# Attention on one Trainium2 core: three key banks, one bank for values and sums, and row maxima carried by two DMAs through DRAM

## The reference

```python
q = (layernorm(x) @ Wq + bq)          # heads of 32, scaled by 32 ** -0.5
k = (ctx @ Wk + bk);  v = (ctx @ Wv + bv)
attn = softmax(clip(q @ k.T, -1e4, 1e4))
x = x + tanh(g_xattn) * ((attn @ v) @ Wo + bo)
x = x + tanh(g_ffn) * (h + 0.5 * (silu(norm(h) @ w1 + b1) @ w2 + b2))   # h = layernorm(x); w1, w2 dequantised
```

## Time and profile before

| | us |
|---|---|
| Median of 3 runs | 3423.44 (3421.34 to 3423.89) |
| The profiled execution, its own time | 3422.4 |
| Its span in the profile | 3420.6 |
| First and last turn of row maxima (L708) | 491.0 and 2439.3 |
| PE busy over the span | 3212.1 (94%) |
| DVE / ACT / POOL busy over the span | 2032.0 / 1603.2 / 1909.7 |

### The profile page before, as it was taken

How to read it: one execution, slowest core, us unless ns; L and a number is a source line. 1 busy time by engine, 2 the same in 40 slices (tenths; PEclk the granted TensorE clock), 3 DMA queues, 4 the chain that set the end, 5 groups by cost and what they waited for, 6 DMA issues and landing times. The chain is left out here.

```text
span 3420.6 us, 51826 instructions
## 1 busy us (share of the span) xinstructions
PE 3212.1 (94%) x15941; PEld 1871.3 (55%) x15941; DVE 2032.0 (59%) x2788; ACT 1603.2 (47%) x2847; POOL 1909.7 (56%) x897
## 2 busy tenths in 40 slices
PE   6799979999999999999999999999656699999999
PEld 5688844444444444444444444444244588888887
DVE  8766656666666666666666666666469433333332
ACT  2222226666666666666666666666522111111111
POOL 4666537777777777777777777777554000000000
PEclk9899979999999999999999999999978899999999
DMA  5566672212222122212222122221195100000000
GB/s 170 187 209 213 213 223 57 56 39 54 56 56 51 42 56 56 55 46 47 56 56 55 41 53 56 56 51 43 57 279 176 40 25 25 25 25 25 15 14 22
DMA packets 142086, 263.11 MB, mean 77 GB/s; under 512 B 16961, under 2 KB 57921, under 8 KB 134721
## 3 DMA queue, kind: packets, MB, share of 16 engines
q1 hardware_dynamic: 141344, 253.82, 26.1%
q10 hardware_dynamic: 672, 8.39, 0.8%
HBM read 168.84 MB, written 93.32 MB: 77 GB/s over the span
## 5 line engine op out<-in xcount | busy, mean ns | idle before, releaser
L852 DVE TENSOR_REDUCE at_half_max<-ps 128x1 f32<-128x1024 f32 x1024 | 1245.0, 1225 | 635.0 <-PE ps L671 623.3
L790 ACT ACTIVATE at_probT<-ps 128x512 f32<-128x512 f32 x2048 | 1113.2, 595 | 418.6 <-PE ps L688 364.4
L620 POOL TENSOR_TENSOR at_gp_sum<-at_gp_sum,at_probT 128x1024 f32<-128x1024 f32 x512 | 1218.3, 2380 | 42.4
L671 PE MATMUL ps<-at_k_stack,at_q_stack 96*128 96x512 f32 x2048 | 868.2, 425 | 19.8 <-DMA at_k_stack<-kT_hi 18.2
L688 PE MATMUL ps<-at_q_stack,at_k_stack 98*128 98x512 f32 x2048 | 876.8, 429 | 9.3 <-ACT at_probT L790 3.4
L671 PEld LDWEIGHTS ps<-at_k_stack,at_q_stack 96*128 96x128 f32 x2048 | 390.1, 191 | 392.9 <-DVE at_half_max L852 202.0
L688 PEld LDWEIGHTS ps<-at_q_stack,at_k_stack 98*128 98x128 f32 x2048 | 385.8, 189 | 351.2 <-ACT at_probT L790 319.1
L615 POOL TENSOR_TENSOR at_gp_sum<-at_probT 128x1024 f32<-128x1024 f32 x128 | 304.9, 2382 | 431.9 <-ACT at_probT L790 431.9
L725 PE MATMUL ps<-at_probT,at_v_head 128*32 128x512 f32 x4096 | 542.4, 601 | 0.9 <-ACT at_probT L790 0.9
L1361 ACT ACTIVATE ff_y<-ps,ff_b_t 128x512 f32<-128x512 f32 x128 | 88.2, 689 | 612.8 <-PE ps L1324 612.8
L1376 POOL TENSOR_TENSOR ff_x_in<-ff_x_in,ff_b_half 128x2048 f32<-128x2048 f32 x8 | 36.8, 4602 | 601.6 <-DVE ff_x_in L1398 601.6
(11 more groups left out here) (154 smaller groups left out, 3890.2 us busy)
## 6 DMA issues: line engine op xcount, KB each, us to landing
at_k_stack<-kT_hi SPq DMA_DIRECT2D x128, 256.0 KB, 4.9
kT_hi<-kv_k_hi SPq DMA_DIRECT2D x16, 1024.0 KB, 4.2
kT_lo<-kv_k_lo SPq DMA_DIRECT2D x16, 1024.0 KB, 6.5
v_heads<-kv_v_out SPq DMA_DIRECT2D x16, 1024.0 KB, 5.7
at_q_stack<-qT_hi SPq DMA_DIRECT2D x128, 128.0 KB, 3.3
at_k_stack<-kT_lo SPq DMA_DIRECT2D x64, 256.0 KB, 4.3
at_v_head<-v_heads SPq DMA_DIRECT2D x64, 256.0 KB, 5.0
kv_c_in<-in_ctx_dram SPq DMA_DIRECT2D x16, 768.0 KB, 7.1
```

Of the source, the lines that this page charges most:

```text
L620: pool.tensor_tensor(gp_sum[lane % 2][:, :, :], gp_sum[lane % 2][:, :, :], pairs[:, 2 * i + 2:2 * i + 4, :], ALU.add).then_inc(gp_added, 1)
L671: mm = pe.matmul(ps[:, n, :], q_stack[buf][0:PARTS, rows], k_stack[buf][0:PARTS, BANK * n:BANK * (n + 1)], start=True, stop=True)
L790: act.activation(probT[lane % 2][:, kv, :], src, ACT.Exp).then_inc(exp_done, 1)
L852: dve.tensor_reduce(dst, src, AX_X, ALU.max).then_inc(max_done, 1)
```

## The change

Four things change in `attend`, on the path without clipping:

1. Key products take turns on three banks, 4, 5 and 6, in place of two. Each waits for the exponential of the key product three before it.
2. Values and sums share bank 7. Two rounds of `values` stand in one slot (C) and two in the next (D). `fold` and three of the sums (`fold_values`) stand in the next slot A, and the last three sums in the slot B after it. There are as many of these products as before.
3. The turn of the row maxima on TensorE and the copy on ScalarE are gone. SP writes `neg_hi` to a DRAM tensor, element by element (128 partitions x 8 elements of 4 bytes), waits until that has landed, and issues a second DMA that reads it back as 2 rows of 512 elements into `q_stack`. The first key product of the unit waits for that DMA (`row_loaded`).
4. The key products of a unit begin one slot later than before (`KEYS` 7 in place of 6). `attend` runs one slot more at its end.

```diff
-    TURN, KEYS, PV, FOLD = 5, 6, 7, 12
+    TURN, KEYS, PV, SUMS, FOLD = 6, 7, (10, 11), 12, 13
+    RING = 3
+    def key_bank(lane, kv):
+        return 4 + (KVT * lane + kv) % RING
...
+            def turn_maxima(head, slot, half):            # on SP
+                unit = HALVES * head + half
+                sp.wait_ge(split_done, 5 * (unit + 1))
+                sp.dma_start(neg_d[bass.ds(unit, 1)].rearrange("u t b p -> p (u t b)"),
+                             neg_hi[:, :, :].bitcast(F32).rearrange("p t b -> p (t b)"), allow_slow_non_contiguous=True).then_inc(neg_moved, 16)
+                sp.wait_ge(neg_moved, 16 * (unit + 1))
+                rows = q_stack[slot][PARTS:PARTS + 2, BANK * half:BANK * (half + 1)]
+                sp.dma_start(rows.bitcast(F32).rearrange("b (t p) -> b t p", p=P),
+                             neg_d[bass.ds(unit, 1)].rearrange("u t b p -> b (u t) p")) \
+                    .then_inc(row_loaded, 16)
...
+                if (n := at(base, slot, 2, BUFS, N_HEADS)) is not None:
+                    turn_maxima(n, (slot - 2) % BUFS, 1)   # after the loads of a head
...
+                if (n := at(base, slot, 1, BUFS, N_HEADS)) is not None:
+                    turn_maxima(n, (slot - 1) % BUFS, 0)   # after the stores of a head
...
-                    pe.wait_ge(row_copied, unit + 1)
-                need(pe, exp_done, KVT * unit + kv - 1)
+                    if clipping:
+                        pe.wait_ge(row_copied, unit + 1)
+                    else:
+                        pe.wait_ge(row_loaded, 16 * (unit + 1))
+                need(pe, exp_done, KVT * unit + kv - RING + 1)
...
-                need(act, fold_done, unit)
-                act.copy(partial[:, :], ps[:, 6, :]).then_inc(partial_done, 1)
+                need(act, partial_read, unit)
+                act.copy(partial[:, :], ps[:, 7, :]).then_inc(partial_done, 1)
...
             def step(base, slot):                          # TensorE
                 scores(base, slot, 0)
                 keys(base, slot, 0)
                 scores(base, slot, 1)
                 keys(base, slot, 1)
-                fold(base, slot)
-                for r in range(QT):
-                    values(base, slot, PV + r, (r,))
+                spread_maxima(base, slot)                  # with clipping alone
+                values(base, slot, PV[0], (0, 1))
+                values(base, slot, PV[1], (2, 3))
+                fold_values(base, slot)
                 last_sums(base, slot)
-                turn_maxima(base, slot)
                 scores(base, slot, 2)
                 keys(base, slot, 2)
                 scores(base, slot, 3)
                 keys(base, slot, 3)
```

More of the change, by code:

```diff
@@ L582, in attend @@
         split_done = sem("split_done")
+        neg_moved = sem("neg_moved")
+        row_loaded = sem("row_loaded")
         row_turned = sem("row_turned")
@@ L683, in keys, with spread_maxima @@
                 if kv == 0:
-                    pe.wait_ge(row_copied, unit + 1)
-                need(pe, exp_done, KVT * unit + kv - 1)
+                    if clipping:
[3 more added lines that the diff above has]
+                need(pe, exp_done, KVT * unit + kv - RING + 1)
                 q = BANK * (lane % HALVES)
-                pe.matmul(ps[:, 4 + kv % 2, :],
+                pe.matmul(ps[:, key_bank(lane, kv), :],
                           k_stack[buf][0:rows, P * kv:P * (kv + 1)], q_stack[buf][0:rows, q:q + BANK],
                           start=True, stop=True).then_inc(tile_done, 1)
-            def turn_maxima(base, slot):
+            def spread_maxima(base, slot):
                 unit, lane, r = unit_at(base, slot, TURN)
-                if unit is None or r:
+                if unit is None or r or not clipping:
                     return
@@ L701, in turn_maxima @@
                     cols = slice(P * t, P * (t + 1))
[L702 to L709, removed]
+                    for part in range(2):
+                        mm = pe.matmul(ps[:, 7, cols], wide[:, part, t, :], ident_r[:, :],
+                                       start=(part == 0), stop=(part == 1))
                 mm.then_inc(row_turned, 1)
@@ L721, in values @@
                     pe.wait_ge(v_loaded[buf], 16 * n_loads + 16)
-                    need(pe, partial_done, unit)
+                    need(pe, gather_done, unit)
+                    if clipping and not (isinstance(unit, int) and unit + 1 >= UNITS):
+                        pe.wait_ge(row_copied, unit + 2)
                 for r in rounds:
                     for g in range(4):
-                        mm = pe.matmul(ps[D * g:D * (g + 1), 6, :], v_head[buf][:, 4 * r + g, :],
+                        mm = pe.matmul(ps[D * g:D * (g + 1), 7, :], v_head[buf][:, 4 * r + g, :],
                                        probT[lane % 2][:, 4 * r + g, :], start=(r == 0), stop=(r == QT - 1))
@@ L728, in values, with fold_values, last_sums @@
                     mm.then_inc(pv_done, 1)
-            def last_sums(base, slot):
-                unit, lane, r = unit_at(base, slot, PV + QT - 1)
+            def fold_values(base, slot):
+                unit, lane, r = unit_at(base, slot, SUMS)
                 if unit is None or r:
                     return
-                need(pe, gather_done, unit)
+                pe.wait_ge(partial_done, unit + 1)
+                pe.matmul(ps[0:D, 7, :], A["fold"][:, :], partial[:, :], start=True, stop=True)
                 for g in range(1, 4):
-                    pe.matmul(ps[D * g:D * (g + 1), 7, :], ones[:, :], probT[lane % 2][:, KVT - 5 + g, :],
-                              start=True, stop=False)
-            def fold(base, slot):
+                    mm = pe.matmul(ps[D * g:D * (g + 1), 7, :], ones[:, :], probT[lane % 2][:, KVT - 5 + g, :],
+                                   start=True, stop=False)
+                mm.then_inc(partial_read, 1)
+            def last_sums(base, slot):
                 unit, lane, r = unit_at(base, slot, FOLD)
@@ L793, in copy_maxima @@
                 unit, lane, r = unit_at(base, slot, TURN)
-                if unit is None or r:
+                if unit is None or r or not clipping:
                     return
                 act.wait_ge(row_turned, unit + 1)
[L797 to L803, removed]
+                need(act, shift_done, KVT * (unit - 1))
+                act.copy(neg_rows[lane % 2][:, :], ps[:, 7, :]).then_inc(row_copied, 1)
             def copy_partial(base, slot):
-                unit, lane, r = unit_at(base, slot, PV + QT - 1)
+                unit, lane, r = unit_at(base, slot, PV[1])
                 if unit is None or r:
@@ L867, in split_maxima @@
                     need(dve, row_turned, unit)
+                    need(dve, neg_moved, 16 * unit)
                     dve.tensor_scalar(neg_hi[:, :, 0], row_max[:, :], -1.0, None, ALU.mult).then_inc(split_done, 1)
@@ L878, in split_maxima @@
                     dve.tensor_reduce(neg_pair[:, :, 1].bitcast(F32R), pair, AX_X, ALU.max).then_inc(split_done, 1)
-                    need(dve, row_turned, unit)
+                    need(dve, neg_moved, 16 * unit)
                     dve.tensor_reduce(neg_hi[:, :, 0], pair, AX_X, ALU.max, negate=True).then_inc(split_done, 1)
```

14 lines of the change are left out of this document (8 added, 6 removed).

## The result

The changed kernel takes 4149.68 us (median of 4 runs, 4143.28 to 4158.2) against 3423.66 of the kernel before: 1.2124 times the time, 95% interval 1.2099 to 1.2148. I had forecast 3289, faster, with a range of 3264 to 3352. It is slower by 726 us, beyond even the 3690 of the rival that I had put on that side.

A forecast was written before the change was run, and what follows sets the result against it. PE was taken as the bound, losing time to two key banks. -1.0 (ring), -0.24 (turn) and +0.16 (VectorE) a unit, times 128, plus 4 us for start and end, gave 3289 us; range 3264 to 3352.

The forecast's parts named there:

- Where PE loses time before: Between s0 and s1 of every slot, two key banks make PE lose 0.25 us, 1.0 us a unit.
- the wait for VectorE in front of slot B: s0 of slot B waits for VectorE's first maximum of slot A, which has only 3.11 us; +0.16 us a unit.
- slots C and D: With two groups of values or sums each, these slots take 4.00 us each.
- the start: First unit's maxima go out while weights still arrive: 0 to 3 us, taken as 1.
- Three key banks: Key products in every slot no longer wait for ScalarE's exponentials: -1.0 us a unit, bounds 0 and -1.0.
- The turn on TensorE, values and sums: Removing the turn (L708) saves 0.24 us a unit; values and sums move between slots at 0 cost.
- The time allowed for the DMAs: From the end of VectorE's small reductions in slot A to k0 of slot D: 8.67 us.
- The time needed: Two landings in series before k0 of slot D: 2.9 us each, 6.0 in all, hidden by 2.7.
- The upper bound: Round trip at two of the slowest 4-byte-piece landings, 2 x 5.8 us, with semaphores 11.8 us.
- Rival 1: Dear 4-byte writes delay k0 of slot D; a loss from 9.8 us, 3690 us at 11.8; chance 0.07.
- Rivals 3 and 4: 3: stall moves to k1 or slot A, 3353 us, chance 0.11; 4: third bank does nothing, 3417, chance 0.02.

The follow-up runs named there:

- write32: The changed kernel with its first DMA writing 128 pieces of 32 bytes, maxima landing in the wrong order; 3289.1 us.
- ring_turn: The changed kernel without the two DMAs: row maxima turned by TensorE and copied by ScalarE again, as a 17th tile in the key-bank ring; 3317.22 us.
- busy_wait: The changed kernel with 18 extra products, their results overwritten, before the wait of the unit's first key product for the second DMA; 3890.94 us.
- spread64: The changed kernel writing its 1024 pieces of 4 bytes 64 bytes apart, the second DMA reading query projection rows instead; 3291.9 us.
- half4: The changed kernel writing only the first of two parts, 512 adjacent pieces of 4 bytes, second DMA reading query projection rows; 3936.7 us.

## Why the prediction was wrong

**Where PE loses time before: right.** With the round trip hidden (`write32`) the period is 14.29 against 14.26, and the total 3289.1 against 3289. That the total agrees to 0.1 us is in part luck. From 1000 to 1500 us the wait for VectorE in front of slot B costs 0.30 a unit (0.19 before s0, 0.10 behind it), where 0.16 was booked; slots C and D take 3.93, where I had 4.00; and the first k0 of all waits 5.9 us for its rows, where 1 was booked for the start.

**Three key banks: right.** s0 to s1 takes 0.47, but for slot B, where 0.57 is the mean in `write32`, after the wait for VectorE. Key products of `write32` waited for ScalarE 19 times, against 1018 before. The ring is worth 0.84 in `ring_turn` where my 1.0 and the 0.16 of VectorE together give 0.84.

**The turn on TensorE, values and sums: right.** 14.49 in `ring_turn` and 14.29 in `write32` differ by 0.20; the turn was booked at 0.24.

**The time allowed for the DMAs: right.** 8.67 worked out, 8.57 in the trace.

**The time needed: here the prediction failed.** I wrote 2 x 2.9 + 0.2 = 6.0 between bounds of 4.4 and 11.8. It is 13.05 in the unit shown. The term that is off is the first landing, the write: 2.9 in the sum, 10.5 in the median. The second, the read, was right: 2.9 in the sum, 2.6 in the median. The upper bound failed too, and for a plain reason: it was taken from a transfer that *reads* DRAM in 4-byte pieces. I had written that no row shows a 4-byte write, and yet used the reads to choose a value near the lower end. (They also give 0.3 us for 1024 pieces, and not 0.2: 0.5 us for 1536 more. It changes nothing.) The reads said nothing of writes: 1024 adjacent pieces take about three times as long to land as the same number 64 bytes apart.

**The clock: missing.** Every rival was priced with its wait alone. At a wait of 4.5 us the price is 6.5, since PE ran at half its clock after it. With the measured wait and without the clock I would have come to 3288 + 4.54 x 128 = 3869; the clock's 259 (`busy_wait`) brings 4128, the measured 4150 less 22.

**The rivals.** Rival 1 is what happened, with its place (k0 of slot D) and its point of decision (9.8 us) right, its price of 401 us too low for both reasons, and its chance of 0.07 far too low. The Trainium skill's rule that transfers under 512 B are done as read-modify-write (DMA: Bandwidth & Descriptors, Specifications), which I had named and weighed lightly, points the same way as the trace of this kernel, but it does not give the size: `spread64` and `write32` are under 512 B too, and land after 3.2 and 1.9 us. What sets the price here is whether pieces of 4 bytes are adjacent: 10.5 us against 3.2 at 64 bytes apart. The fixed cost of about 2 us that I had taken from the Trainium skill (same page, section Anatomy of one DMA) is given there for DMAs issued by GpSimd; SP issues these, and 1.9 of `write32` is near it. Rivals 3 and 4 did not happen.

## What to carry to other kernels

A price that the trace does not show needs its bound from the same direction of transfer, source and target: a read in small pieces bounds no write in small pieces. Where two transfers in series stand in front of the bounding engine, work out the slack first, and if it is smaller than a pessimistic landing, the edit is a bet on that one number, to be measured by itself before the rest is built on it. Price a wait of several microseconds in front of TensorE with the halved clock behind it.

## What the runs showed that I had not expected

- A DMA that writes 1024 adjacent 4-byte pieces to DRAM keeps the DMA engines busy for about 0.5 us and lands 9 to 12 us after its issue. The DMA share in the profile is 0.00 in between, so neither it nor the bytes (4 KB) warn of it.
- The same number of pieces 64 bytes apart: 2.2 to 4.1 us between the issues. 128 pieces of 32 bytes: 1.4 to 3.4. Both ranges are without the first unit, whose write took 10.7 us or more in every version; weights are still arriving then.
- The two landings are not independent. In those 38 units of the changed kernel k0 started 12.7 to 13.7 us after the first issue, though the second landing alone took from 1.5 to 4.4: a late first one is followed by a short second. The unit at 1524 is of the one kind, this one of the other:

```profile
996.91 0.39 SPq L643 DMA_DIRECT2D minus_maxima<-at_neg_hi  x1
1008.52 0.27 SPq L647 DMA_DIRECT2D at_q_stack<-minus_maxima  x1
```

```profile
1010.08 0.77 PE L720 MATMUL ps<-at_q_stack,at_k_stack 98*128 98x512 f32 x1 [4.58 <-DMA at_q_stack<-minus_maxima]
```

- `half4`, whose second DMA reads another tensor, does the same, at 10.9 to 12.1 us in 24 units. So it is not the reading of the bytes just written; the cause stays open.
- 18 useless products in front of a wait made the kernel 259 us faster, by keeping the granted clock at 1.00.
- Why adjacent writes of 4 bytes land so late is not settled by these runs. They show that adjacency counts for much more than the number: half as many adjacent pieces took 8.5 us in place of 10.5, the same number spread out 3.2.
